# Graph layer plus routed feed-forward layer on one core: another order of work in the opening and in the first feed-forward group, and a second feed-forward product that comes out with rows on the partitions

## The reference, cut to what matters

```python
x = x + gnn(layernorm(x), adj)         # 8 batches of 1024 nodes, 128 features
x = x + ffn(layernorm(x))
# gnn: two convolutions along the nodes (1 and 17 taps, batch norms folded),
#      A = exp(-dist) * adj, A @ relu(x @ w_msg.T + b_msg), a GRU cell
# ffn: weights = x @ wr + br; the 511 heaviest rows of each batch are taken,
y = gelu(sel @ w1 + b1) @ w2 + b2      # 128 -> 512 -> 128 features
y = y * w_sel                          # each row times its own router weight
return processed + x                   # y set at the rows taken, 0 elsewhere
```

## Time and profile before

| | us |
|---|---|
| median of 3 runs (lowest, highest) | 564.93 (564.66, 565.52) |
| the profiled execution | 564.87 |
| its span, first to last instruction | 562.3 |
| PE busy | 545.6 (97%) |
| VectorE busy | 475.0 (84%) |
| ScalarE busy | 354.9 (63%) |
| GpSimd busy | 275.7 (49%) |

### The profile page before, as it was taken

How to read it: one execution, slowest core, us unless ns; L and a number is a source line. 1 busy time by engine, 2 the same in 40 slices (tenths; PEclk the granted TensorE clock), 3 DMA queues, 4 the chain that set the end, 5 groups by cost and what they waited for, 6 DMA issues and landing times.

```text
span 562.3 us, 9026 instructions
## 1 busy us (share of the span) xinstructions
PE 545.6 (97%) x2964; PEld 416.6 (74%) x2964; DVE 475.0 (84%) x1048; ACT 354.9 (63%) x616; POOL 275.7 (49%) x346
## 2 busy tenths in 40 slices
PE   7799999999999999999999999999999999899996
PEld 3786798678966896689767986798678966666663
DVE  6987478679898989899898989899979987978722
ACT  4856475856686577747674857575856673555552
POOL 2740354325358344834484546654545365536552
PEclk9999999999999999999999999999999999899999
DMA  8602700180008300650047001800171006402111
GB/s 274 278 2 76 300 0 2 45 308 23 2 0 270 142 2 1 193 220 1 1 124 289 1 2 52 323 2 1 46 283 46 1 1 191 148 16 81 36 36 61
DMA packets 33339, 54.52 MB, mean 97 GB/s; under 512 B 2098, under 2 KB 23051, under 8 KB 33166
## 3 DMA queue, kind: packets, MB, share of 16 engines
q1 hardware_dynamic: 29710, 48.42, 24.7%
q0 software_dynamic: 3584, 5.54, 2.8%
HBM read 44.21 MB, written 13.43 MB: 103 GB/s over the span
## 4 chain that ended last, share of the span: by engine, by line
PE 86%; DVE 8%; ACT 3%; DMA 2%; issue 1%; SPq 0%; DVEq 0%; ACTq 0%
PE N L1504 20%; PE M L1481 10%; PE C L1355 7%; PE C L1357 7%; PE C L1356 7%; PE D L1475 5%; PE N L1609 5%; PE N L1355 4%; PE N L1356 3%; PE N L1357 3%; ACT hab L674 2%; DVE tr L1014 2%; PE M L1356 2%; PE M L1355 2%; PE M L1357 2%; PE D L1355 2%
## 5 line engine op out<-in xcount | busy, mean ns | idle before, releaser
L780 ACT ACTIVATE tr<-D 128x512 f32<-128x512 f32 x128 | 76.4, 597 | 76.9 <-PE D L1475 75.2
L1481 PEld LDWEIGHTS M<-cst,adjb 128*128 128x128 f32 x512 | 63.9, 141 | 35.2 <-issue 21.2
L1475 PE MATMUL D<-V,U 128*128 128x512 f32 x128 | 89.3, 698 | 0.0
L1481 PE MATMUL M<-cst,adjb 128*128 128x128 f32 x512 | 76.8, 273 | 0.6 <-DVE ga L1101 0.6
L578 POOL DMA_INDIRECT sel<-R,ridx x56 | 61.1, 1090 | 16.0 <-issue 14.0
L1504 PE MATMUL N<-ga,msgF 128*128 128x512 f32 x128 | 64.2, 594 | 0.0
L1504 PE MATMUL N<-tz,msgF 128*128 128x512 f32 x128 | 64.2, 594 | 0.0
L1355 PE MATMUL C<-zR,wc 128*128 128x256 f32 x208 | 60.6, 291 | 0.6 <-DVE zR L1023 0.6
L1356 PE MATMUL C<-zR,wc 128*128 128x256 f32 x208 | 58.7, 282 | 0.0
L1357 PE MATMUL C<-zR,wc 128*128 128x256 f32 x208 | 58.6, 282 | 0.0
L1131 DVE TENSOR_SCALAR_CACHE_REDUCE junk<-W,R 128x1024 bf16<-128x1024 f32 (+3 forms) x64 | 51.7, 808 | 3.9 <-ACT W L742 3.9
(11 more groups left out here) (236 smaller groups left out, 1527.6 us busy)
## 6 DMA issues: line engine op xcount, KB each, us to landing
adjb<-in_adj SPq DMA_DIRECT2D x8, 4096.0 KB, 14.9
adjb<-sel SPq DMA_DIRECT2D x7, 516.0 KB, 5.3
xall<-in_x SPq DMA_DIRECT2D x7, 512.0 KB, 5.2
out<-R SPq DMA_DIRECT2D x7, 512.0 KB, 3.5
R<-in_conv_w SPq DMA_DIRECT2D x1, 1088.0 KB, 8.6
sel<-R,ridx POOLq DMA_INDIRECT x56
xall<-in_weights SPq DMA_DIRECT2D x1, 832.0 KB, 11.0
xall<-in_x SPq DMA_DIRECT2D x2, 256.0 KB, 2.9
```

Source lines behind the costliest of these rows:

```text
L780: nc.scalar.activation(E[:, u % NE, :], Db[u % NH][:, :], ACT.Exp, scale=-1.0).then_inc(exp_ok, 1)
L1475: MM(Db[h][:, :], U[:, t * P:(t + 1) * P], V[:, half(h)], start=True, stop=True).then_inc(d_ps, 1)
L1481: i = TR(Mb[h][:, k * P:(k + 1) * P], adjb[:, h * TH + k, t * P:(t + 1) * P], ident)
```

## The change

1. *First layer norm.* Moments, small instructions and power are done per half of the tiles.
2. *Opening.* GpSimd waits, between `differences(0, 0)` and `pairs_of_taps`, until VectorE has made the low part of the five shared taps. In `conv1` PE runs the two products with the high part before it waits for the low part.
3. *Second product.* `down` takes 128 of the GELU's columns as weights and `w2` as the moving operand, four times per block, so the result has rows on the partitions. `update` and `update_back` are gone; `updated_rows` reads the product's bank. PE now waits for VectorE's `O_ok` of two groups ago before it reuses that bank.
4. *Bias.* `biased_rows` adds weight times `b2` to the base rows ahead, four VectorE instructions per group, eight more in `last_biased`. A copy of `b2` on all partitions comes by a DMA of its own.
5. *First group.* Its transposes move into the last GRU half, into bank M0, its high part on ScalarE ahead of that half's gates, its low part on VectorE ahead of rank 5. `lo_of_sel(1, 1)` moves between ranks 6 and 7. `state_back` moves behind the third `down`. The three `up` banks are taken in another order.

```diff
         f1_ps, g_ok, f2_in = sem("f1_ps"), sem("g_ok"), sem("f2_in")
-        wmsg_in = sem("wmsg_in")
+        wmsg_in, b2_in = sem("wmsg_in"), sem("b2_in")
         blank_ok, blank_out = sem("blank_ok"), sem("blank_out")
-        y_ps, y_ok, yb_ps, O_ok = sem("y_ps"), sem("y_ok"), sem("yb_ps"), sem("O_ok")
+        y_ps, O_ok, biased = sem("y_ps"), sem("O_ok"), sem("biased")
         out_done = [sem("out_done0"), sem("out_done1")]
         place_ok, kept_ok, last_out = sem("place_ok"), sem("kept_ok"), sem("last_out")
-        up_banks = (C0, C1, D1)
+        up_banks = (D1, C0, C1)
         LU = len(up_banks)
+        def sel_bank(b):
+            return M0 if b == 0 else D0
         def wait(eng, s, b, per, k):
...
             sp.dma_start(cst[:, :], const).then_inc(cst_in, 16)
-            sp.dma_start(vec[:, 0:N_LOADED], vectors).then_inc(vec_in, 16)
+            sp.dma_start(vec[:, 0:V_F2R], vectors[:, 0:V_F2R]).then_inc(vec_in, 16)
             sp.dma_start(raw_w[:, 0:W_IH], weights[:, 0:W_IH]).then_inc(w_in, 16)
...
             sp.dma_start(wmsg[:, :], weights[:, W_MSG:W_MSG + D]).then_inc(wmsg_in, 16)
+            sp.dma_start(b2row, vectors[:, V_F2R:]).then_inc(b2_in, 16)
             load_x(1)
...
             def inv_std0():
-                pool.wait_ge(agg, 1)
                 for h, done in ((0, rstd0_ok), (1, rstd_ok)):
+                    pool.wait_ge(agg, h + 1)
                     ts = slice(h * TH, (h + 1) * TH)
...
                 if first:
+                    pool.wait_ge(wL_ok, W_SC + 1)
                     pairs_of_taps()
...
                 nc.scalar.activation(tz[:, h, :], z[:, :], ACT.Tanh, bias=col(V_GB + 1), scale=0.5).then_inc(tz_ok, 1)
+            def hi_of_sel(b, p):
+                wait(act, t_ps, b, 1, 1)
+                nc.scalar.activation(xTH[:, 0, half(p)], sel_bank(b)[:, :], ACT.Copy).then_inc(xsH_ok, 1)
             def candidate(b, h):
...
                 candidate(b, 0)
+                if last:
+                    hi_of_sel(0, 0)
                 gates(b, 1)
             over_batches(act, step)
-            def hi_of_sel(b, p):
-                wait(act, t_ps, b, 1, 1)
-                nc.scalar.activation(xTH[:, 0, half(p)], D0[:, :], ACT.Copy).then_inc(xsH_ok, 1)
             def gelu(b, p, j):
...
                                      bias=col(V_F1 + j)).then_inc(g_ok, 1)
-            def update(b, p):
-                wait(act, y_ps, b, 1, 1)
-                wait(act, yb_ps, b - 2, 1, 1)
-                nc.scalar.activation(Y[:, p, :], Nb[p][:, :], ACT.Identity, bias=col(V_F2)).then_inc(y_ok, 1)
             def ffn_step(b, q, first, last):
-                if first:
-                    hi_of_sel(0, 0)
                 gelu(b, q, 0)
...
                     candidate(B - 1, 1)
+                gelu(b, q, 1)
+                if first:
                     hi_of_sel(1, 1)
-                gelu(b, q, 1)
                 gelu(b, q, 2)
...
                     row_of_weights(B - 1, 0, M1)
-                if not first:
-                    update(b - 1, 1 - q)
                 gelu(b, q, 3)
...
             over_groups(ffn_step)
-            update(NG - 1, (NG - 1) % 2)
         @block.vector
...
             TS, TT, STT = nc.vector.tensor_scalar, nc.vector.tensor_tensor, nc.vector.scalar_tensor_tensor
+            def moments1_of(b, ts):
+                for t in ts:
+                    nc.vector.bn_stats(st[:, 0, t, :], xall[:, b % NX, t, :]).then_inc(stats1, 1)
             def moments1(b):
...
                     dve.wait_ge(rstd_ok, b)
-                for t in range(T):
-                    if b == 0 and t % TH == 0:
-                        dve.wait_ge((x0_in, x_in[0])[t // TH], 16)
-                    if b > 0 and t == 0:
-                        dve.wait_ge(x_in[b % 2], 16 * (b // 2 + 1))
-                    nc.vector.bn_stats(st[:, 0, t, :], xall[:, b % NX, t, :]).then_inc(stats1, 1)
+                dve.wait_ge(x_in[b % 2], 16 * (b // 2 + 1))
+                moments1_of(b, range(T))
+            def moments0(h):
+                dve.wait_ge((x0_in, x_in[0])[h], 16)
+                moments1_of(0, range(h * TH, (h + 1) * TH))
+                mean_and_variance(0, stats1, (h + 1) * TH, slice(h * TH, (h + 1) * TH), h)
             def moments2(b):
...
                     nc.vector.bn_stats(st[:, 1, t, :], xall[:, b % NX, t, :]).then_inc(stats2, 1)
-            def mean_and_variance(k, stats, n):
-                (me, mo), (ve_, vo) = ((st[:, k, :, i], st[:, k, :, i + 3]) for i in (1, 2))
+            def mean_and_variance(k, stats, n, ts, turn):
+                (me, mo), (ve_, vo) = ((st[:, k, ts, i], st[:, k, ts, i + 3]) for i in (1, 2))
...
                 if last:
+                    lo_of_sel(0, 0)
                     rank(b - 1, 0, 5)
...
                 STT(kept[:, :], rankF[:, :], float(KEEP), R[:, 1, :, R_W], ALU.is_lt, ALU.mult).then_inc(kept_ok, 1)
-            def last_rows(b, h):
-                wait(dve, yb_ps, b, 1, 1)
+            def biased_rows(b):
+                dve.wait_ge(sel_in[b], 16)
+                if b == 0:
+                    dve.wait_ge(b2_in, 16)
+                for c in range(TH):
+                    xs = Xs[:, b, c, :]
+                    STT(xs[:, D:2 * D], b2row, xs[:, R_W:R_W + 1], xs[:, D:2 * D], ALU.mult, ALU.add).then_inc(biased, 1)
+            def last_biased():
                 dve.wait_ge(base_ok, B)
                 dve.wait_ge(kept_ok, 1)
+                for t in range(T):
+                    base = R[:, 1, t, D:2 * D]
+                    STT(base, b2row, kept[:, t:t + 1], base, ALU.mult, ALU.add).then_inc(biased, 1)
+            def last_rows(b, h):
+                wait(dve, y_ps, b, 1, 1)
+                dve.wait_ge(biased, TH * NXS + T)
                 for c in range(TH):
...
                     base = R[:, 1, t, D:2 * D]
-                    STT(base, M0[:, c * P:(c + 1) * P], kept[:, t:t + 1], base, ALU.mult, ALU.add).then_inc(O_ok, 1)
+                    STT(base, Nb[b % 2][:, c * P:(c + 1) * P], kept[:, t:t + 1], base, ALU.mult, ALU.add).then_inc(O_ok, 1)
             def updated_rows(b, p):
...
                     return
-                wait(dve, yb_ps, b, 1, 1)
+                wait(dve, y_ps, b, 1, 1)
+                dve.wait_ge(biased, TH * (b + 1))
                 if b > 1:
...
                     xs = Xs[:, b, c, :]
-                    STT(O[:, p, c, :], M0[:, c * P:(c + 1) * P], xs[:, R_W:R_W + 1], xs[:, D:2 * D], ALU.mult,
+                    STT(O[:, p, c, :], Nb[p][:, c * P:(c + 1) * P], xs[:, R_W:R_W + 1], xs[:, D:2 * D], ALU.mult,
                         ALU.add).then_inc(O_ok, 1)
...
                     new_gate(B - 1, 1)
-                    lo_of_sel(0, 0)
                     rank(B - 2, 0, 6)
+                    lo_of_sel(1, 1)
                     rank(B - 2, 0, 7)
...
                     blend(B - 1, 1)
-                    lo_of_sel(1, 1)
                     state_to_nodes(B - 1, (M1, N1))
                     moments2(B - 1)
-                    mean_and_variance(1, stats2, T * B)
+                    mean_and_variance(1, stats2, T * B, slice(0, T), NH)
                 elif not last:
...
                     rank(B - 1, 1, 3 * (b - 2))
+                if b < NXS:
+                    biased_rows(b)
                 if not first:
...
                     kept_weights()
+                if b == NXS - 1:
+                    last_biased()
             over_groups(ffn_step)
...
                 for h in range(NH):
+                    w, hs = weight(W_C1), half(h)
+                    wait(pe, xTH_ok, b, NH, h + 1)
+                    MM(Db[h][:, :], w(0), xTH[:, q, hs], start=True, stop=False)
+                    MM(Db[h][:, :], w(1), xTH[:, q, hs], start=False, stop=False)
                     wait(pe, xTL_ok, b, NH, h + 1)
-                    three(Db[h][:, :], weight(W_C1), xTH[:, q, half(h)], xTL[:, q, half(h)],
-                          True, True).then_inc(c1_ps, 1)
+                    MM(Db[h][:, :], w(0), xTL[:, q, hs], start=False, stop=True).then_inc(c1_ps, 1)
             def embedding(b, q):
...
                 i.then_inc(c2_ps, 1)
+            def sel_to_features(b):
+                if b < NXS:
+                    pe.wait_ge(sel_in[b], 16)
+                else:
+                    pe.wait_ge(xn2_ok, B)
+                if b == 0:
+                    pe.wait_ge(tr_ok, NH * (B - 1) + 1)
+                if b == 1:
+                    pe.wait_ge(q2_ok, NH * (B - 1) + 1)
+                wait(pe, xsL_ok, b - 1, 1, 1)
+                for c in range(TH):
+                    rows = Xs[:, b, c, 0:D] if b < NXS else R[:, 1, (b - NXS) * TH + c, 0:D]
+                    i = TR(sel_bank(b)[:, c * P:(c + 1) * P], rows, ident)
+                i.then_inc(t_ps, 1)
             def state_back(b, bank_):
...
                 three(nh[:, :], wh(2), *X, True, True).then_inc(gate_ps, 1)
+                if last and h == 1:
```

(51 more changed lines are left out.)

25 lines of the change are left out of this document (11 added, 14 removed).

## The result

The changed kernel took 569.13 us (median of 4, 568.52 to 570.01) beside 565.14 us for the kernel before: ratio 1.0077, 95% interval 1.0064 to 1.0091. Forecast were 565.9 us and a range up to 567.6. The profiled execution took 570.01 us, span 568.2. Measured again later, the same program gave two more answers: 566.38 us beside 564.19 (ratio 1.0034, interval 1.0022 to 1.0047), and 575.76 us beside 564.70 (ratio 1.0194). So there are two questions: what the change does, and what makes one program differ by more than 9 us.

What follows compares the result with a forecast made beforehand. PE was taken to bound the kernel, with 86% of the chain. 564.87 + 1.9 (GpSimd's wait) + 1.5 (low clock) - 2.4 (feed-forward stage) = 565.9 us, range 563.0 to 567.6.

Steps and rivals of the forecast that it cites:

- The step that failed: Feed-forward from the ups of group 6 to the end: PE alone sets the pace, -2.7 us in all.
- Norm by halves: Opening, first layer norm: first transposes some 0.4 us earlier, but ScalarE then waits for the taps' DMA; value 0.
- GpSimd's wait: Opening: VectorE and GpSimd take turns, pair sums end at 20.95, conv_even_common starts at about 27.4; +1.9 us.
- Low clock: Opening: PE idles 4.1 us before conv_even_common, then the clock is low for some 3.4 us; +1.5 us.
- rival 1: Opening: clock falls while PE still waits, so a second low stretch follows; another 1.5 us, 567.4 in all; chance 12%.
- `down` at 0.112 us: Feed-forward second product: one 128-column instruction per 0.112 us, 0.895 a block, +0.14 us a group.
- First group, VectorE's queue: Start of the feed-forward stage: VectorE's work delays the first group, lo_of_sel(2) at 500.9 instead of 501.52.
- VectorE's pace in groups 1 to 4: Feed-forward: each group adds 1.04 us of bias less idle time; PE starts group 6's ups +0.35 us later.
- PE-bound periods: Feed-forward after group 4: PE bounds, each group 0.3 us shorter, two periods -0.6.
- Tail: Last group, down 0 to last_rows: 3.83 us instead of 5.57, as the last update_back and ScalarE step go; -1.74.
- Rival 5: Feed-forward `down`: weight loads show, fifteen PE-bound blocks longer by up to 0.62 us each; 575 us; chance 2%.

Runs made afterwards that it cites:

- the undisturbed profile: The changed kernel unaltered, measured a third time, with no GELU late beyond the very first: 566.38 us, ratio 1.0034.
- e2: The kernel before with only GpSimd's new wait for the low part of the first taps: 568.71 us beside 564.43, ratio 1.0078.
- e17: The changed kernel with the old opening and biased_rows of groups 1 and 2 straight behind lo_of_sel: 561.72 us, ratio 0.995.
- e5: The changed kernel unaltered, measured a second time: 575.76 us beside 564.70 for the kernel before, ratio 1.0194.

## Why the prediction was wrong, by its steps

**The step that failed.** The prediction took PE's completions to reach ScalarE at once, as they always did in the kernel before, and so let PE alone set the pace from the ups of group 6 to the end: two periods and the rest of group 7 shorter, and the tail, -2.7 in all. In the first measurement's profile this stretch is 1.4 us longer than before (536.90 to 568.2 against 532.38 to 562.3), because the increments of the ups reached ScalarE up to 4.1 us late and PE then stood still for 3.14. In the undisturbed profile it is 2.9 shorter. What delays them stays open. Ahead of it, in the same first profile, the opening cost 2.75 (forecast 3.4) and the stage up to group 6 1.8 (forecast 0.35; undisturbed 1.04).

**The other steps**, by the undisturbed profile (span 563.96, first exp at 35.62):

- *Norm by halves, 0*: wrong beside GpSimd's wait. With `conv1`'s order it brought VectorE to the shared taps at 15.66 instead of the 16.31 forecast, and 0.5 us of the wait went (e2 against the full change).
- *GpSimd's wait, +1.9*: the mechanism was right to 0.4 us (pair sums end 20.5, forecast 20.95). `conv_even_common` starts 1.36 later. In e2, without those two edits and with a low clock in `conv1`, it was 2.7.
- *Low clock, +1.5*: right that it falls, too small here. The level was already low when `conv_even_common` started, in this profile (from 24.9) and in the first one (from 26.6). That is the sign the prediction named for its rival 1, two low stretches at 3.0 in all. Here it lasted 6.8 us, twice the 3.4 of the kernel before, as rival 1 has it, and cost 2.1; in the first profile it lasted 3.4 and cost 1.35, as the forecast has it. So the truth lies between the two and changes from execution to execution. The opening came to +3.5, forecast +3.4: two errors that cancel.
- *`down` at 0.112 us*: right (eight in 1.05 with the last one's 0.27).
- *First group, VectorE's queue*: `lo_of_sel(2)` at 501.0 after taking off the opening's 3.5, forecast 500.9. Right.
- *VectorE's pace in groups 1 to 4, +0.35 at the ups of group 6*: too small. 536.92 less 3.5 is 533.42, +1.04. I counted idle times as given back that the bias, by its place behind the first rank, could not use in full: the low parts of groups 3, 4 and 5 came 0.8, 1.2 and 1.4 us later, forecast 0.5, 0.5 and 0.7. This is the term of the sum that was mis-sized, by 0.7 us; moving the instructions (e17) gave 1.05 back.
- *PE-bound periods*: 6.89 and 6.88 us, -0.33 each, forecast -0.3. *Tail*: `last_rows` 3.77 behind `down` 0, forecast 3.83; -1.80, forecast -1.74. Right.

With these the sum is 562.3 + 3.5 + 1.04 - 0.66 - 0.33 - 1.80 = 564.05 against a span of 563.96. That the undisturbed median of 566.38 lies in the forecast's own range is partly luck. Beside the kernel before (564.19 in that series) it is +2.2, where the forecast had +1.0; the forecast started from a profiled execution at 564.87, 0.7 above that median.

What put the first measurement outside every range, 569.13, is the failed step. None of the rivals had it: rival 1 adds time in the opening only, and that was not longer than forecast in the first profile. Rival 5 names nearly the 575.76 us of e5, but its mechanism, weight loads that show, is refuted by the 0.112.

## To carry to other kernels

Added work on a full engine costs by its place in the queue: put it into the idle time that a wait there leaves, before moving it to another engine. A wait that orders two engines on the opening's critical path costs twice, once in time and once in the clock behind PE's idle. And when one program gives 566 and 576 us, look in the chain for "issue" and at waits released by "remote" before explaining the median.

## What the hardware showed that I had not expected

- One program in two kinds of execution, 566.4 against 569.1 and 575.8 us, with 89 to 100 increments of PE, VectorE and ScalarE missing from the record in the slower kind and PE's increments reaching ScalarE up to 4.4 us late, at nearly fixed places in the program.
- An idle of 3.97 to 3.99 us in one program was followed by 3.4 us of low clock in one execution and 6.8 us in another, both times with the fall ahead of PE's resumption.
- A float32 matmul of 512 columns over one row of weights costs no less than over 128: 1.06 us to the next matmul, where the full block took 0.86.
- VectorE and GpSimd took turns also in the new order: 2.20 and 1.74 us for pair sums of 1.45.
